# Two mixture-of-experts stages: the first stage's shared expert moved behind the routed blocks and its logits in plain fp32, the second stage's results added into two tensors in memory

## The reference, cut to what matters

```python
x = x + tanh(g_xattn[0]) * L0_xattn(layernorm(x), ctx, ctx)
x = x + tanh(g_ffn[0])   * L0_ffn(layernorm(x))      # 32 experts of width 128, top 8 within 4 of 8 groups
x = x + tanh(g_xattn[1]) * L1_xattn(layernorm(x), ctx)
x = x + tanh(g_ffn[1])   * L1_ffn(layernorm(x))      # 8 experts of width 256, top 2

# L0_ffn: scores = sigmoid(flat @ gate_w.T), normalised over the chosen 8; L1_ffn: softmax, top 2 of scores + bias
out    = sum_e combine[:, e] * ((silu(flat @ wg_e.T) * (flat @ wu_e.T)) @ wd_e.T)
shared = (silu(flat @ sg.T) * (flat @ su.T)) @ sd.T   # every token; width 128 in L0, 512 in L1
# L1_xattn: feats = [enc, hq_hat, enc * hq_hat, enc * hc_bar];  out = feats @ W_qv + b_qv
```

## Time and profile before

| | us |
|---|---|
| median of 3 runs | 1169.85 (1169.49 to 1174.03) |
| the profiled execution | 1170.15 |
| its span, first to last instruction | 1168.3 |
| PE busy (78% of the span) | 905.8 |
| DVE busy (60%) | 699.6 |
| POOL busy (43%) | 507.0 |
| ACT busy (38%) | 439.2 |

### The profile page before, as it was taken

The page is one execution under the profiler, slowest core; times in us unless marked ns, Lnnn a source line. Parts: engine busy times, 40 slices in busy tenths (PEclk is TensorE's granted clock), DMA queues, the critical chain, the costliest instruction groups (busy, mean ns, idle before and its releaser), DMA issues.

```text
span 1168.3 us, 20181 instructions
## 1 busy us (share of the span) xinstructions
PE 905.8 (78%) x5388; PEld 687.2 (59%) x5389; DVE 699.6 (60%) x2031; ACT 439.2 (38%) x1033; POOL 507.0 (43%) x572
## 2 busy tenths in 40 slices
PE   3568888867378999999997018799999977998920
PEld 2457777755244888888886004456565735886710
DVE  6779999986834875555554246757673353443322
ACT  4558888954122344444443002131314031232200
POOL 7255655634002755555551777757000003322055
PEclk9689999989555999999999558899998987999965
DMA  8940000012001776777676634333000021334234
GB/s 244 224 84 2 0 0 0 1 53 89 1 0 28 214 214 203 216 229 216 204 177 143 246 98 137 113 109 111 15 1 18 1 73 54 105 116 133 87 106 132
DMA packets 65640, 122.59 MB, mean 105 GB/s; under 512 B 10449, under 2 KB 41426, under 8 KB 65426
## 3 DMA queue, kind: packets, MB, share of 16 engines
q0 software_dynamic: 17184, 46.95, 15.4%
q1 hardware_dynamic: 21426, 48.62, 13.9%
q10 hardware_dynamic: 26944, 25.96, 6.5%
HBM read 80.33 MB, written 32.24 MB: 96 GB/s over the span
## 4 chain that ended last, share of the span: by engine, by line
PE 58%; DVE 18%; issue 7%; DMA 6%; POOL 4%; ACT 3%; SPq 1%; DVEq 0%; POOLq 0%; ACTq 0%
PE bank L941 17%; PE bank L956 8%; PE bank L1617 5%; PE bank L1578 4%; POOL yg L1224 4%; DVE ptl L625 4%; PE bank L930 4%; PE bank L823 3%; DVE nmax L617 3%; PE bank L1551 2%; DMA sw<-in_w 2%; PE bank L949 2%; PE bank L435 2%; PE bank L1516 2%; DMA yg<-slot_rows,slot_of 2%
## 5 line engine op out<-in xcount | busy, mean ns | idle before, releaser
L1208 POOL DMA_INDIRECT xg<-token_rows,gather_idx x198 | 188.3, 951 | 384.2 <-DVE gather_idx L1375 217.3
L941 PE MATMUL bank<-sw,xgt 128*128 x948 | 246.2, 382 | 0.2 <-issue 0.2
L1224 POOL DMA_INDIRECT yg<-slot_rows,slot_of x160 | 163.6, 1023 | 116.9 <-DMA slot_rows<-ysb 60.6
L941 PEld LDWEIGHTS bank<-sw,xgt 128*128 128x128 f32 x948 | 166.0, 192 | 15.5 <-issue 1.0
L1051 ACT ACTIVATE ssil<-bank 128x128 f32<-128x128 f32 x237 | 65.7, 277 | 222.8 <-PE bank L941 222.8
L956 PE MATMUL bank<-sw,sht 128*128 x474 | 143.7, 385 | 0.0
L1143 DVE COPY xgt<-bank 128x256 f32<-128x256 f32 x198 | 83.7, 423 | 79.7 <-PE bank L930 71.0
L1156 DVE COPY sht<-bank 128x128 f32<-128x128 f32 x237 | 69.0, 291 | 103.1 <-PE bank L949 102.4
L553 ACT ACTIVATE prob<-bank,nmax 128x256 f32<-128x256 f32 x256 | 111.4, 510 | 6.5 <-DVE nmax L617 6.5
L435 PE MATMUL bank<-consts,prob 128*128 128x128 f32 x512 | 83.5, 288 | 35.7 <-DVE ptl L625 33.2
L1239 DVE SCALAR_TENSOR_TENSOR x<-yg,gate_of,x 128x256 f32<-128x256 f32 x160 | 65.6, 478 | 73.4 <-DMA yg<-slot_rows,slot_of 73.4
(11 more groups left out here) (225 smaller groups left out, 1529.4 us busy)
## 6 DMA issues: line engine op xcount, KB each, us to landing
slot_rows<-ysb ACTq DMA_DIRECT2D x98, 256.0 KB, 3.3
sw<-in_w SPq DMA_DIRECT2D x48, 384.0 KB, 3.4
kst<-khl SPq DMA_DIRECT2D x32, 224.0 KB, 5.1
token_rows<-xn SPq DMA_DIRECT2D x8, 512.0 KB, 3.2
xg<-token_rows,gather_idx POOLq DMA_INDIRECT x198, 3.4
yg<-slot_rows,slot_of POOLq DMA_INDIRECT x160, 2.8
x<-in_x SPq DMA_DIRECT2D x4, 512.0 KB, 5.1
craw<-in_ctxt SPq DMA_DIRECT2D x4, 512.0 KB, 6.4
```

What stands on the lines that cost most here:

```text
L941: mm = pe.matmul(bank[2 + k % 2][:, 0:2 * FF], xgt[:, i % 3, c * P:(c + 1) * P], w[:, :, c, :], start=(c == 0), stop=(c == CH - 1))
L1208: nc.gpsimd.indirect_dma_start(xg[:, (first + i) % XG_RING, 0:ROW[L]], None, rows[L], bass.IndirectOffsetOnAxis(gather_idx[:, i:i + 1], 0) ...
L1224: nc.gpsimd.indirect_dma_start(yg[:, t % Y_TILES, j, :], None, ybuf[L], bass.IndirectOffsetOnAxis(slot_of[:, t, j:j + 1], 0)).then_inc(s_y ...
```

## The change

Front 0 loses all splitting. The turned x is copied once (`x_copied`), and the logits are 32 plain fp32 matmuls that give them by token. The shared expert of stage one becomes `shared0_*`: after the last routed block the four batches are turned again and go through plain fp32 gate, up and down matmuls, ahead of DVE's first gated addition. `weights` stands behind `indices`.

In the second attention the bias row is scaled once and added to x by DVE (`bias_added`), and in batch 1 `attended_normalised(0)` stands behind the first two row maxima. In the routing of stage two the exponentials stand ahead of the SiLUs, all tables behind `shared_gate_up(3, 3)`.

Stage two's result rows are scaled by their gate as they leave PSUM. The gates reach the slots as eight more columns of `token_rows1`, stored from `cw` in 2048 pieces of 32 bytes, for which the first gather waits. GpSimd adds each block to `token_sums0` or `token_sums1` in turn, by a scattering DMA with add; each waits for the one before it on the same tensor. Slots without a token go to 128 spare rows. SyncE clears both tensors during batch 1 of the second attention, and loads them at the end in 8 DMAs. `shared_down(3)` and `shared_added(3)` stand behind the sparse stage.

```diff
 # front 0, TensorE (splits, silu, hidden, hidl, add of the shared expert are removed likewise on ACT, DVE, POOL)
-                for c in range(CH):
-                    for wp in range(2):
-                        for xp in (xh, xl):
-                            mm = pe.matmul(bank[4][0:ne, :], rwhl[:, c, wp * ne:(wp + 1) * ne],
-                                           xp[:, c, b * SEQ:(b + 1) * SEQ], start=(n == 0), stop=(n == 7))
+                pe.wait_ge(m.xh, 2 * b + 2)
+                    for c in range(CH):
+                        mm = pe.matmul(bank[5][:, t * E0:(t + 1) * E0], xt[:, b % 2, c, j * P:(j + 1) * P], rraw[:, c, :],
+                                       start=(c == 0), stop=(c == CH - 1))
...
-            down(3)
-            table(pe, 0, m, range(8, TILES))
+            table(pe, 0, m, range(TILES))
             expert_row(pe, 0, m)
+
+        def shared0_tensor(pe, m):
...
+            def gate_up(b):
+                pe.wait_ge(m.xh, 2 * BATCH + 2 * (b + 1))
+                if b:
+                    pe.wait_ge(m.h, b)
+                for half, ready in ((0, m.gate), (1, m.up)):
+                    for c in range(CH):
+                        w = slice((CH * half + c) * FF, (CH * half + c + 1) * FF)
+                        mm = pe.matmul(bank[half][:, :], wsh0[:, w], xt[:, b % 2, c, :], start=(c == 0), stop=(c == CH - 1))
+                    mm.then_inc(ready, 1)
...
+            pe.wait_ge(m.wload, 16)
+            pe.wait_ge(s_sye, BLOCKS[0])
+            turned(0)
+            turned(1)
+            for b in range(BATCH):
+                gate_up(b)
+                if b + 2 < BATCH:
+                    turned(b + 2)
+                if b:
+                    down(b - 1)
+            down(BATCH - 1)
...
 # stage two, ScalarE
+            def y_gated(i, e):
+                act.wait_ge(s_sy, UNITS + first + halves * (i + 1))
+                if i >= 2 * Y_RING:
+                    act.wait_ge(s_scat[i % 2], 16 * ((i - 2 * Y_RING) // 2 + 1))
+                nc.scalar.activation(ysb[:, i // 2 % Y_RING, i % 2, :], bank[6 + i % 2][:, 0:DIM], ACT.Copy,
+                                     scale=xg[:, (first + i) % XG_RING, bass.ds(DIM + e, 1)]).then_inc(s_sye, 1)
...
 # stage two, GpSimd
+        def scattered(pool, i):
+            pool.wait_ge(s_sye, FIRST[1] + i + 1)
+            if i >= 2:
+                pool.wait_ge(s_scat[i % 2], 16 * (i // 2))
+            nc.gpsimd.indirect_dma_start(
+                total[i % 2], bass.IndirectOffsetOnAxis(scatter_idx[:, i:i + 1], 0), ysb[:, i // 2 % Y_RING, i % 2, :],
+                None, compute_op=ALU.add).then_inc(s_scat[i % 2], 16)
...
+            for i in range(BLOCKS[L] + LAG * L):
+                if L == 1 and i >= LAG:
+                    scattered(pool, i - LAG)
...
 # SyncE
+            if L == 1:
+                sp.wait_ge(m.cw, m.n["cw"] + 1)
+                sp.dma_start(rows[1].rearrange("(t p) c -> p t c", p=P)[:, :, DIM:DIM + E1], cw[:, :, 0:E1]).then_inc(m.rows, 16)
...
+                if b == 1:
+                    sp.wait_ge(s_zero, 1)
+                    for i in range(2):
+                        rows_of = total[i].rearrange("(p a) c -> p a c", a=TILES + 1)
+                        sp.dma_start(rows_of, zeros[:, :].unsqueeze(1).broadcast_to([P, TILES + 1, DIM])).then_inc(s_cleared, 16)
...
+            for i in range(2):
+                sp.wait_ge(s_scat[i], 16 * len(range(i, BLOCKS[1], 2)))
             for b in range(BATCH):
-                sp.wait_ge(s_yadd, TOP0 * TILES + TOP1 * TPB * (b + 1))
+                for i in range(2):
+                    by_tile = total[i][0:TOKENS, :].rearrange("(t p) c -> p t c", p=P)
+                    sp.dma_start(sums[:, b, i], by_tile[:, TPB * b:TPB * b + TPB, :]).then_inc(s_sum[b], 16)
+            for b in range(BATCH):
+                sp.wait_ge(s_yadd, TOP0 * TILES + 2 * b + 2)
                 sp.dma_start(out[:, b * TPB:(b + 1) * TPB, :], x[:, b * TPB:(b + 1) * TPB, :]).then_inc(s_out, 16)
...
 # second attention
-                            if g == 1:
-                                pe.matmul(o, ones1[0:1, :], bqv1[:, :], start=True, stop=False)
+                nc.vector.tensor_tensor(x[:, ts, :], x[:, ts, :], bqvg[:, :].unsqueeze(1).broadcast_to([P, TPB, DIM]),
+                                        ALU.add).then_inc(A["bx"], 1)
...
                 maximum(b, 1)
+                if b == 1:
+                    attended_normalised(b - 1)
                 normalised(b, 0)
```

More of the change, by code:

```diff
@@ L92, in gated_xattn_moe_kernel @@
         ybuf = [nc.dram_tensor(f"slot_rows{L}", (BLOCKS[L] * SLOTS, DIM), F32).ap() for L in range(2)]
+        total = [nc.dram_tensor(f"token_sums{i}", (TOKENS + P, DIM), F32).ap() for i in range(2)]
         a0 = ExitStack()
@@ L1041, in front0_scalar, with shared0_scalar, turned_copied, silu @@
-            hidden_hi(3)
             hots_by_token(act, 0, m, range(TILES))
+        def shared0_scalar(act, m):
+            def turned_copied(b):
+                for c in range(CH):
+                    act.wait_ge(m.tr, 2 * BATCH + 2 * b + c + 1)
+                    nc.scalar.activation(xt[:, b % 2, c, :], bank[2 + 2 * (b % 2) + c][:, :], ACT.Copy).then_inc(m.xh, 1)
+            def silu(b):
+                act.wait_ge(m.gate, b + 1)
+                nc.scalar.activation(hid1[:, b, :], bank[0][:, :], ACT.Silu).then_inc(m.sil, 1)
+            turned_copied(0)
+            turned_copied(1)
+            for b in range(BATCH):
+                silu(b)
+                if b + 2 < BATCH:
+                    act.wait_ge(m.up, b + 1)
+                    turned_copied(b + 2)
@@ L1077, in sparse_scalar, with shared0_vector, hidden, add @@
                     y_copied(i)
-            for q in range((blocks - 1) // 2, PAIRED[L]):
-                store(q)
+            if L == 0:
+                for q in range((blocks - 1) // 2, PAIRED[0]):
+                    store(q)
         def front0_vector(dve, m, first, routing, tables):
             ranked, weights, hots, indices = tables
-            def add(v):
-                dve.wait_ge(m.y, v + 1)
+            ln_norm(dve, 1, 0, m.xn)
+            ln_norm(dve, 1, 1, m.xn)
+            ln_norm(dve, 1, 2, m.xn)
+            dve.wait_ge(s_xa, 2 * TILES)
+            ln_stats(dve, 1, 3)
+            ln_norm(dve, 1, 3, m.xn)
+            first()
+            for part in routing:
+                part()
+            ranked()
+            hots(range(TILES))
+            indices()
+            weights()
+        def shared0_vector(dve, m):
+            def hidden(b):
+                dve.wait_ge(m.up, b + 1)
+                dve.wait_ge(m.sil, b + 1)
+                nc.vector.tensor_tensor(hid1[:, b, :], hid1[:, b, :], bank[1][:, :], ALU.mult).then_inc(m.h, 1)
+            def add(b):
+                dve.wait_ge(m.y, b + 1)
                 for j in range(TPB):
-                    t = TPB * v + j
+                    t = TPB * b + j
                     op = nc.vector.scalar_tensor_tensor(
@@ L1662, in tensor_a1, with shared_down, shared_added @@
             shared_gate_up(b, 2)
-            table(pe, 1, m, range(0, 8))
             shared_gate_up(b, 3)
-            table(pe, 1, m, range(8, TILES))
+            table(pe, 1, m, range(TILES))
             expert_row(pe, 1, m)
-            shared_down(b)
+        def shared_down(pe, m, b):
+            pe.wait_ge(m.h, m.n["h"] + SH1 * (b + 1))
+            if b == BATCH - 1:
+                pe.wait_ge(m.acc, m.n["acc"] + TPB * b)
+                pe.wait_ge(s_sye, FIRST[1] + BLOCKS[1])
+            for j in range(TPB):
+                for u in range(SH1):
+                    mm = pe.matmul(bank[6 + j // 2][:, (j % 2) * DIM:(j % 2 + 1) * DIM], hid1[:, u, j * P:(j + 1) * P],
+                                   wsh1[:, u, 2 * CH * FF:WCOLS], start=(u == 0), stop=(u == SH1 - 1))
+            mm.then_inc(m.y, 1)
+        def shared_added(dve, m, b):
+            dve.wait_ge(m.y, m.n["y"] + b + 1)
+            for j in range(TPB):
+                t = TPB * b + j
+                nc.vector.scalar_tensor_tensor(
+                    out=x[:, t, :], in0=bank[6 + j // 2][:, (j % 2) * DIM:(j % 2 + 1) * DIM],
+                    scalar=tg[:, 3:4], in1=x[:, t, :], op0=ALU.mult, op1=ALU.add).then_inc(m.acc, 1)
         def scalar_a1(act, m):
@@ L1887, in vector_a1 @@
             first()
+            routing[0]()
+            routing[1]()
             shared_hidden(b, 0)
-            for part in routing:
-                part()
+            routing[2]()
             shared_hidden(b, 1)
@@ L1991, in _ @@
             sparse_vector(dve, 1, moe[1])
[L1992 to L1993 removed]
+            shared_added(dve, moe[1], BATCH - 1)
+            dve.wait_ge(moe[1].acc, moe[1].n["acc"] + TILES)
+            for b in range(BATCH):
+                dve.wait_ge(s_sum[b], 32)
+                for i in range(2):
+                    if i:
```

(3 more changed lines are left out.)

383 lines of the change are left out of this document (130 added, 253 removed).

## The result

The changed kernel takes 1106.02 us (median of 4 runs, 1102.8 to 1108.6) where the kernel before took 1169.67 beside it: ratio 0.9449, 95% interval 0.9412 to 0.9486. The forecast was 1096 with a range of 1080 to 1135. The profiled execution took 1107.14 us, with a span of 1105.3; 63.0 less than before, where the sum said 73.7. Stretches are read from single profiled executions; ratios are from the timed runs.

A forecast was written before the change was run, and what follows sets the result against it. Several limits: TensorE in stage one's blocks and front 0's table, with time to be had in front 0, the gap behind stage one and the tail. -30.4 + 0 - 14.5 - 7.7 + 1.0 - 22.1 = -73.7 gives 1096 us, range 1080 to 1135.

The forecast's parts named there:

- Front 0: Up to `gather_idx` of stage one: weight load, splits and `down` work leave the chain, written at 338.7 instead of 369.1, 30.4 us saved.
- The lower bound, 26: Front 0's saving in us if the logit instructions take 0.29 each and the transposes double.
- Stage one's shared expert: Behind stage one's blocks: TensorE's work is hidden by POOL's gathers, cost 0; 29 us if that cover were gone.
- Rival B: Behind stage one: cover fails, TensorE drops to clock 0.50 for the shared expert, 14 us late, 1110 us; chance 0.10.
- Second attention: Bias matmuls gone from TensorE and maxima first in batch 1: 14.5 us saved, 9 to 18.
- Routing of stage two: Tables ready earlier, shared_down gone from here, gates' store taken as 6 us: 7.7 saved, at the other end 8 lost.
- Rival C: Routing of stage two: gates' store takes 21.4 us, the 7.7 gain becomes 8 lost, 1112 us; chance 0.14.
- Stage two's blocks: The 39 blocks keep TensorE's pace; register load and more traffic beside the weights put at 1 us lost.
- S: Time of one scattering addition in stage two: taken as 4.5 us, between 3.4 (a gather) and 6.8 (with a second leg).
- Tail: Behind the last block: copy, issue, scatter, loads and additions take 29.6 us instead of 51.7, 22.1 saved.
- Rival A: Stage two: scattering additions pace it if above 6.8 us, 1198 at 12; chance 0.09 mild, 0.07 beyond 10.6.
- Rival D: Front 0's table runs at full clock, DVE's 1.2 to 1.3 per tile binds, 16 us less, 1080; chance 0.06.

The follow-up runs named there:

- table_outer: Changed kernel with normalisation first in batch 1, stage two's gates ahead of the ranks, and only hot_hi and its column numbers stored copies-outermost, DVE following: 1093.55 us.
- one-sum run: Changed kernel with all 39 scattering additions into one of the two sums, each waiting for the one before: 1151.0 us, ratio 0.9813.
- warm_table: Changed kernel with TensorE kept busy in front 0 by matmuls whose result nobody reads, nothing taken away: 1126.91 us, ratio 0.961.
- unit_stride: Changed kernel with both table operands, hot_tok and hot_hi, stored with the eight copies outermost, ACT and DVE writing with the stride: 1182.2 us, ratio 1.0076.
- table_pairs: As `table_outer`, but hot_hi and its column numbers stored with pairs of copies innermost: 1090.95 us, ratio 0.9309.
- plain_scatter: Changed kernel with scatters that overwrite instead of adding; number, size, order and waits stay: 1098.67 us, ratio 0.9369.

## Why the prediction was right, point by point

The total was right because each of the four gains is a chain of waits that the change cut, and the chain named the same work in both traces. The sum was 10.7 us too low. That it was not further off is in part luck: the routing and the tail came out 8.3 us better than forecast, the other stretches together 19.0 worse. By its own steps:

- **Front 0** (-30.4, came out -28.1). Load, splits and `down` instructions went as costed, and the last normalisation ended at 269.6 (268.2 forecast). The logits behind the last transposes were miscounted and mis-sized: I took 16 instructions for 2.5 us, but the list of calls has `x_transposes(pe, m, 3)`, `logits(2)`, `logits(3)`, which is 32, and at 0.21 each (clock 0.50) they take 6.68. In this trace TensorE is at 0.50 from 258 on, so even the transposes and logits before them are the chain. In `table_outer`, at clock 1.00 from 262 to 266, DVE's last normalisation is the chain as forecast, and the last 32 logits still take 6.68 at the low clock. Why the clock is lower here than in the kernel before is not shown. The lower bound, 26, was drawn for this case, and the result lies inside it.
- **Stage one's shared expert** (0): the run without it shows 0 within 0.2 us. Rival B did not happen, at clock 1.00.
- **Second attention** (-14.5, came out -8.5). Two terms failed. The bias was 8.7 and is 6.7 by the batches (4.7 by the ratio): I had batches 1 to 3 bound by TensorE, but in batch 1 TensorE waits for DVE, and the gain there is next to nil. The reordering was 5.8 of gain and is about 3 of loss (63.0 us for batch 1 against 59.8): I let the wait of 5.13 us vanish because something else filled the place, but DVE's work had only changed its order, and the next consumer waited. The 8.5 of the traces less 6.7 plus 3.2 leaves 5.0 us of gain. Of these 3.3 go with TensorE's clock in batches 2 and 3: before the change the first gate and up instructions of the shared expert in batch 2 took 5.23 us (clock 0.66 from 825 to 830), and the logits and those instructions of batch 3 3.12 and 5.71 (0.59 and 0.62); in the changed kernel they took 3.54, 1.95 and 5.23 (1.00, 1.00 and 0.67). The run with the bias matmul has this gain too, and the trace without stage one's shared expert has lost the half in batch 2 (57.5 us instead of 55.9), so it is no term of the change that a run shows. The rest stays open; it is less than two traces of the changed kernel differ by.
- **Routing of stage two** (-7.7, came out -10.6). The store was mis-sized, 2.95 us for 6. I had divided a queue's time by its packets; q10's were of 963 bytes and took 45 ns each by that division, while the store's own, of 32 bytes and with no other transfer beside them, took 7 ns by the same division (23.8% of 16 engines over 4 us, 2064 packets). Whether the size or the company makes the difference is not shown. Rival C rested on the same division.
- **Stage two's blocks** (+1.0, came out +7.4) is the step that failed most. S was 3.8 in the median and 3.7 to 4.4 over the 39 (4.5 taken) and the pace did not bind, as forecast: POOL waited for a scatter once, 0.9 us. The upper bound, a second leg as long as the gather, was an estimate: without the addition the median is 2.4, so the addition costs 1.4, and how the DMA makes it is not shown. What I priced at almost nothing was "more traffic beside the weights": the run without the addition is 8.0 us faster, and its trace has 6.8 of them in the stage and 1.4 in the last landing.
- **Tail** (-22.1, came out -27.5): copy, issue and last scatter 1.3 shorter (I had added POOL's issue to S, which holds it), the loads 1.2 shorter, 3.1 instead of 6.0 us behind the last addition.
- **Rival A**: the one-sum run shows its mechanism at 4.4 us per scatter. It would have decided at S = 10.6, more than twice the 4.4.
- **Rival D** could not have come true: with this stride the table's matmuls did not depend on the clock (2.28 us for a tile's eight at 1.00, 2.31 at 0.50). I had read the 0.29 us as the low clock's, with no row at the high clock to compare.

## What to carry to other kernels

Price a DMA that adds by what it takes from the other transfers of its stage, not by its own latency: 39 scatters that hardly held anything up (POOL waited 0.9 us for them) still cost 6.8 us of their stage through the weight loads. When a wait goes because work was put in another order on the engine waited for, and none was removed, look for the next consumer and charge it the wait. And when an engine is slow at a low clock, look at its duration at the high clock before blaming the clock: here it was the stride of an operand (2.31 us for eight matmuls at 0.50, 2.28 at 1.00, and 1.29 at 0.50 with the columns side by side).

## What the runs showed of the hardware

- A matmul whose moving operand of 159 fp16 columns is read 16 bytes apart took 0.286 us at clock 1.00 (`warm_table`) and 0.289 at 0.50 (the changed kernel); read contiguously it took 0.16 at 0.50 (`unit_stride`, `table_outer`), and read 4 bytes apart 0.16 at 0.50 and 0.11 at 1.00 (`table_pairs`). No other distances were run.
- Writing fp16 with a stride of 256 or 318 bytes cost ACT 4.7 ns per element (4.86 us for 1024) and DVE 4.5 (5.70 for 1272), four and seven times their contiguous 1.15 and 0.81 us (`unit_stride` against the changed kernel). DVE kept its pace with pairs innermost (0.82, `table_pairs`) but not with an input that stands still along the innermost direction (1.48, `table_outer`).
- POOL's index table of 1272 numbers per partition took 1.42, 2.39 or 7.09 us with rows of 159, of 8 and of 2 (`table_outer`, the changed kernel, `table_pairs`); DVE's four normalisations beside it took 4.05, 5.02 and 9.72, where twelve without an index table beside them took 4.42 in the changed kernel, 1.5 for four. Each time the normalisations took 2.63 us more than the table: what POOL's table took longer, they took longer.
- A scatter of 128 rows of 1 KB: issued in 1.59 us and landed in 3.8 with the addition (medians of the 39 in the changed kernel; 3.7 to 4.4), in 0.99 and 2.4 without (`plain_scatter`; up to 4.2); landing counts from the start of the issue.
